# Splitting the first half of each expert's scatter-addition into two instructions of 64 rows

## What is computed

```python
feats  = rfs(x, ...);  dense = einsum('bsr,or->bso', feats, weights)
# after a router (64 experts, 8 per token) and a normalization, per expert e:
dispatch[e, slot] = tokens[token of that slot]                 # up to 256 slots
g, u = dispatch @ gate_w, dispatch @ up_w
expert_out = (silu(g) * u) @ down_w
output = zeros.at[token].add(expert_out[e, slot] * weight)     # scatter-addition
output = output + shared expert + dense + x
```

## Time and profile before

| | |
|---|---|
| Device time, median of 3 runs | 1292.82 us (1292.47 to 1304.77) |
| Span of the profiled execution | 1293.7 us |
| Expert phase, from the first gather to the end | 666.4 to 1293.7 us |
| TensorE busy (share of the span) | 1271.5 us (98%) |
| VectorE, ScalarE, GpSimd busy | 72%, 50%, 33% |
| Instructions L1728 (additions) | 128, 2 for each expert |

### The profile page before, as it was taken

One profiled execution on the slowest core, in us unless ns is written; L12 is line 12 of the kernel. 1 busy time (PEld: TensorE's weight loads), 2 busy tenths in 40 slices (PEclk: granted clock), 3 DMA queues, 4 the chain that ended last, 5 costly groups with the idle time before them and its releaser, 6 DMA issues.

```text
span 1293.7 us, 23014 instructions
## 1 busy us (share of the span) xinstructions
PE 1271.5 (98%) x7585; PEld 1119.3 (87%) x7585; DVE 931.2 (72%) x1853; ACT 646.5 (50%) x1126; POOL 432.8 (33%) x344
## 2 busy tenths in 40 slices
PE   8999999999999999999999999999999999999994
PEld 7888888888888888888889999999999999999993
DVE  7887787867878678785655777777767777777762
ACT  6422223222232223321255777777777777777772
POOL 2000000000000000000013666666676767777754
PEclk9999999999999999999999999999999999999997
DMA  8246554565545655445347999999999999999995
GB/s 312 82 137 169 123 135 104 144 168 125 125 108 146 168 118 128 110 117 136 130 139 202 303 283 301 284 303 290 291 289 300 284 291 303 283 300 290 299 261 69
DMA packets 210969, 263.66 MB, mean 204 GB/s; under 512 B 49268, under 2 KB 137208, under 8 KB 210936
## 3 DMA queue, kind: packets, MB, share of 16 engines
q1 hardware_dynamic: 181464, 191.40, 50.6%
q0 software_dynamic: 28672, 71.32, 24.5%
q10 hardware_dynamic: 800, 0.53, 0.2%
HBM read 178.18 MB, written 71.39 MB: 193 GB/s over the span
## 4 chain that ended last, share of the span: by engine, by line
PE 95%; DMA 2%; issue 1%; POOL 1%; DVE 0%; POOLq 0%; ACT 0%; ACTq 0%
PE pmm L1333 18%; PE pmm L1332 18%; PE pmm L1331 17%; PE pout L1331 11%; PE pout L1333 11%; PE pout L1332 11%; PE ptr L1569 4%; PE plp L1396 2%; DMA out_dram<-outs,slot_cols 1%; POOL out_dram L1728 1%; PE pmm L1587 1%; PE plp L1425 1%; DMA out_dram<-feat,slot_cols 1%; PE plp L1405 1%; PE ptr L1343 0%
## 5 line engine op out<-in xcount | busy, mean ns | idle before, releaser
L1332 PE MATMUL pmm<-xt_lo,proj_hi 128*128 128x256 f32 (+1 forms) x776 | 244.3, 315 | 0.0
L1333 PE MATMUL pmm<-xt_hi,proj_lo 128*128 128x256 f32 (+1 forms) x776 | 244.3, 315 | 0.0
L1332 PE MATMUL pmm<-xt_lo,sgu_hi 128*128 128x256 f32 (+1 forms) x764 | 240.1, 314 | 0.0
L1333 PE MATMUL pmm<-xt_hi,sgu_lo 128*128 128x256 f32 (+1 forms) x764 | 240.0, 314 | 0.0
L1331 PE MATMUL pmm<-xt_hi,proj_hi 128*128 128x256 f32 (+1 forms) x744 | 235.8, 317 | 0.6 <-DVE xt_lo L844 0.6
L1331 PE MATMUL pmm<-xt_hi,sgu_hi 128*128 128x256 f32 (+1 forms) x732 | 231.3, 316 | 0.0
L1712 POOL TENSOR_TENSOR earlier<-earlier,chosen 128x64 bf16<-128x64 bf16 x64 | 24.2, 378 | 610.3 <-DVE chosen L965 606.6
L1718 POOL DMA_INDIRECT xbuf<-rows,slot_cols x128 | 176.0, 1375 | 90.4 <-issue 36.1
L566 ACT ACTIVATE feat<-pmm,ab 128x512 f32<-128x512 f32 x66 | 45.4, 688 | 286.5 <-PE pmm L1333 286.5
L1332 PEld LDWEIGHTS pmm<-xt_lo,proj_hi 128*128 128x128 f32 x776 | 145.7, 188 | 11.4
L1333 PEld LDWEIGHTS pmm<-xt_hi,proj_lo 128*128 128x128 f32 x776 | 145.7, 188 | 10.4
(11 more groups left out here) (214 smaller groups left out, 2630.6 us busy)
## 6 DMA issues: line engine op xcount, KB each, us to landing
raw<-in_L_ffn_gate_w_dram SPq DMA_DIRECT2D x64, 512.0 KB
raw<-in_L_ffn_up_w_dram SPq DMA_DIRECT2D x64, 512.0 KB
raw<-in_L_ffn_down_w_dram SPq DMA_DIRECT2D x64, 512.0 KB
outs<-in_L_attn_x_dram SPq DMA_DIRECT2D x32, 512.0 KB, 4.0
out_dram<-outs SPq DMA_DIRECT2D x32, 512.0 KB, 3.0
xbuf<-in_L_attn_x_dram SPq DMA_DIRECT2D x52, 256.0 KB, 7.5
raw<-xn SPq DMA_DIRECT2D x52, 256.0 KB, 6.2
rows<-raw SPq DMA_DIRECT2D x39, 256.0 KB, 4.2
```

Of the source, the lines that this page charges most:

```text
L1332: pe.matmul(psum, lh, rl, start=False, stop=False)
L1333: ins = pe.matmul(psum, ll, rh, start=False, stop=final and n == len(pairs) - 1)
```

## The change

The first of the two additions of an expert becomes two instructions of 64 rows (source rows in partitions 0 to 63, then 64 to 127); the second stays one instruction of 128 rows. [...] The three instructions raise `added` by 48 for each expert, and the waits on `added` in ScalarE and SyncE are counted anew.

```diff
+ADDS = 3
...
+        upper_cols = sb("upper_cols", [P // 2, E * CB], U32)
...
+            def copy_upper_cols(n):
+
+                sp.wait_ge(slot_cols_made, n + 1)
+                at = bass.ds(CHUNK * CB * n, CHUNK * CB)
+                sp.dma_start(upper_cols[:, at], slot_cols[P // 2:, at]).then_inc(upper_cols_made, 16)
...
             refill_gate_up(turn(3))
+            copy_upper_cols(0)
             refill_down(turn(2))
             with sp.Fori(0, CHUNKS - 3) as m:
                 for k in range(CHUNK):
...
                     if k == 1:
                         load_chunk(m + 3)
+                    if k == 2:
+                        copy_upper_cols(m + 1)
             for n in range(E - 2 * CHUNK, E):
                 refill_gate_up(turn(n))
                 refill_down(turn(n - 1))
+                if n % CHUNK == 2:
+                    copy_upper_cols(n // CHUNK)
             refill_down(turn(E - 1))
-            sp.wait_ge(added, 16 * CB * E)
+            sp.wait_ge(added, 16 * ADDS * E)
...
             def e_out(e):
                 act.wait_ge(slot_w_made, e.n + 1)
-                at_least(act, added, 16 * CB * (e.n - 3))
+                at_least(act, added, 16 * ADDS * (e.n - 3))
...
             def add_rows(e):
-                at_least(pool, added, 16 * CB * e.n)
-                for c in range(CB):
-                    at = CB * e.n + c
-                    pool.wait_ge(e_out_made, at + 1)
+                at_least(pool, added, 16 * ADDS * e.n)
+                if e.n % CHUNK == 0:
+                    pool.wait_ge(upper_cols_made, 16 * (e.n // CHUNK + 1))
+                first, second = CB * e.n, CB * e.n + 1
+                for source, place, index in (
+                        (0, slice(0, P // 2), slot_cols[0:P // 2, first:first + 1]),
+                        (0, slice(P // 2, P), upper_cols[:, first:first + 1]),
+                        (1, slice(0, P), slot_cols[:, second:second + 1])):
+                    pool.wait_ge(e_out_made, CB * e.n + source + 1)
                     pool.indirect_dma_start(
-                        out=out, out_offset=bass.IndirectOffsetOnAxis(ap=slot_cols[:, at:at + 1], axis=0),
-                        in_=e_outs[e.q][c], in_offset=None, bounds_check=last_row,
+                        out=out, out_offset=bass.IndirectOffsetOnAxis(ap=index, axis=0),
+                        in_=e_outs[e.q][source][place], in_offset=None, bounds_check=last_row,
                         oob_is_err=True, compute_op=ALU.add).then_inc(added, 16)
```

More of the change, by code:

```diff
@@ L307, in build @@
         slot_cols_made = sem("slot_cols_made")
+        upper_cols_made = sem("upper_cols_made")
         gu_loaded = [[sem(f"{m}_loaded{b}") for m in ("gate", "up")] for b in range(2)]
```

## The result

The changed kernel takes 1371.13 us (median of 4 runs, 1368.77 to 1374.51), the kernel before 1295.31 us beside it: ratio 1.057, 95% interval 1.053 to 1.061. Slower by 5.7%, or 76 us by the medians; the profiled spans differ by 79.1 us (1372.8 against 1293.7).

What follows compares the result with a forecast made beforehand. GpSimd's loop of additions, through issue and landing, was taken as the bound; 60 turns of +0.64 us (+38.4) plus +3.6 for the last four gave +42, thus 1335 us, range 1291 to 1375.

Steps and rivals of the forecast that it cites:

- the +0.3 to +1.0 that I had given 0.55: Forecast case for the addition loop: each turn longer by +0.3 to +1.0 us, total 1310 to 1357 us, chance 0.55.
- the part that I had given 0.20: Case of a third batch's cost or a 64-row issue price near its upper end: 1357 to 1400 us, chance 0.20.
- my own two signs of being wrong: 64-row issue under 0.85 us, or second addition's landing over 0.5 us sooner after its issue than 5.4 us.
- The bound: GpSimd's loop of additions, bound by issuing and landing latency, sets the time: 9.32 us a turn against TensorE's 9.25.
- The copies at nothing: 16 DMAs of 2 KB on SyncE, about 0.4 us of issue each, covered by waiting time: costed at nothing.
- 60 turns of +0.64 us: Addition loop to expert 60: +0.89 us of issuing less 0.25 gained, a turn of 9.96 us, +38.4 us in all.
- The gain of 0.25 us at the landing: Second addition's landing gains from fewer rows ahead and their earlier start: bounds 0 and 0.5 us, 0.25 taken.
- the slopes within the kernel before: Least-squares line through 55 turns: 0.9 us of turn per us of the second addition's issue, 1.4 per us of the first's.
- The last turns and TensorE's idle time: Last four turns add 3.6 us; TensorE idles about 0.7 us per expert without adding time and ends near 1315.
- Each batch has a start of its own, 1373 us: Rival: a third batch on the queue costs +1.26 us a turn, 76 + 4 us; range 1365 to 1380, within chance 0.20.
- Moving starts sooner: Rival: the first rows' 0.5 us earlier start shortens the turn to 9.07 us; 1283 to 1292 us, chance 0.10.

Runs made afterwards that it cites:

- Two sums: Odd experts add to a second tensor, so an addition waits only for the expert two back: changed kernel so edited 1290.0 us, kernel before so edited 1287.5 us.
- delay before: Kernel before with some 1.7 us of GpSimd fills, moving no data, ahead of each expert's first addition: ratio 1.062 to the kernel before.
- delay between: Kernel before with some 1.7 us of GpSimd fills, moving no data, between each expert's two additions: ratio 1.038 to the kernel before.
- 96 rows: Changed kernel with the first half split into 32 and 96 rows instead of 64 and 64: 1367 us, ratio 1.054 to the kernel before.
- both halves split: Changed kernel with the second half split too, four instructions of 64 rows for each expert: 1412 us, ratio 1.086 to the kernel before.
- light loads: Only the first quarter of gate and up weights loaded from the third expert on: changed kernel so edited 1300.5 us, kernel before so edited 1291.1 us.

## Why the prediction came out as it did

The range held the time (1371 in 1291 to 1375), near its upper end; the forecast of 1335 was 36 us short. The turn of +1.24 us lies above the +0.3 to +1.0 that I had given 0.55, in the part that I had given 0.20. One of my own two signs of being wrong came true as well: B's landing was to come at most 0.5 us sooner, and came 0.9 us sooner than the 5.4 named there.

*The bound.* Right, and shown: the loop of additions through landing sets the time. Two sums take its wait away, and the third instruction then costs 0.2%.

*The copies at nothing.* Right: 1.0005.

*60 turns of +0.64 us.* The step that was mis-sized; measured were +1.24. It had two terms, both too small. The issue of 64 rows was put at 1.1 us, between two bounds of which the upper was nearly true: 1.41 us, fixed price. With the gap that makes 2 x 1.41 + 0.31 - 1.62 = +1.51 of turn and not +0.89. I had read from the cheaper gather that the price goes with something else than the count of rows, and still placed the value nearer to half. Beside this, I priced the issues undisturbed and added nothing for drawn-out ones. The means of the two new issues were 1.72 and 1.98 us, which brings the part ahead of the last issue from 2.07 to 4.31 us, +2.24.

*The gain of 0.25 us at the landing.* Measured 0.99, so this term was too small as well, and my reason for it is not borne out: of the landing itself, 1.01 us sooner, the delay before shows 0.54 us with the additions untouched, and the early start alone (delay between) only 0.15 more. I had taken the slopes within the kernel before, 0.9 and 1.4 us of turn for each us of issue, to hold for a lasting delay too. They are those of a single late turn; the lasting delay before added 1.14 us of turn for 1.81 us of work. The remaining 0.32 us may be the smaller batch ahead of the last; with 96 rows there it landed in 4.48 and not 4.22 us. What shortens the landing in all of these stays open, as said above.

*Luck.* The two errors cancel in part. With the issue part at its measured +2.18 us and the gain left at 0.25, the sum would have been 60 x 1.93 + 3.6 = +119 us, thus 1412, far outside the range. That the range held owes something to this.

*The last turns and TensorE's idle time.* As said: 79.1 less 74 is 5 us in place of 3.6, and TensorE idles 9.8 us in 100, 1.0 us for each expert in place of 0.7, without setting the time. The last output is ready at 1347, not near 1315.

*Each batch has a start of its own, 1373 us.* The right figure by luck, from a mechanism that did not hold: a delay with no third batch costs 50 or 77 us, a third batch without the wait costs 2.5, and with a third batch the last landing comes sooner. (1.4 x 0.89 is 1.25, not 1.26.)

*Moving starts sooner.* It lost. Its bound of 8 us of gain was near: with the coupling gone altogether 1287.5 us, 9.7 us under before.

By the Trainium skill, "DMA: Bandwidth & Descriptors", section "Rules for kernel authors", a split by halves of the partitions should not be bothered with. The outcome agrees, at 1.057; but here the loss came from the issuing engine's nearly fixed price ahead of a wait, and the landing grew no longer by the split.

## What to carry to other kernels

Where an engine waits for the landing of its own last transfer before the next, look for the issue price ahead of that last one: here 1.3 to 1.4 us for an indirect transfer of 32 to 96 rows against 1.6 for 128, so splitting buys nothing, and work moved behind the last issue is nearly free while it fits into the wait. If something must be split in such a loop, split the last transfer and not the first. A slope read from the scatter of single turns is not the price of a lasting change: here 1.81 us of work in each turn made it 1.14 us longer. And do not take the pause before the next issue for the landing where the engine has other work in it; read the landing from its semaphore.

## What the runs showed of the hardware that I had not expected

- The issue of an accumulating indirect transfer: 1.32 us for 32 rows, 1.41 for 64 (1.39 with both halves split), 1.42 for 96, 1.56 for 128, at its shortest.
- A last batch of 64 rows lands about 1 us sooner than one of 128 (waits of 2.4 to 2.7 against 3.4 to 4.1 us, once 4.7, in the last three turns), with no weights loading; half the rows are 128 KB.
- At the same traffic, the last landing comes sooner with three issues for each expert than with two: 4.74 against 5.58 us at 293 GB/s (two sums), 3.45 against 4.85 us at 210 GB/s (light loads). Why is open.
- From 735 to 1230 us of the changed kernel, 54 of the 56 addition issues over 1.72 us overlap one of VectorE's instructions on `raw` (1.23 us in the row shown), 37 of the 85 shorter ones do. No run isolates it.
- GpSimd's fills of a tile began before the indirect issue ahead of them had ended in the profile (1111.05 against 1108.71 + 2.90).
